# Linear attention: the output product of a tile seven turns after its projection, at the end of TensorE's turn, instead of eight turns after it, near the beginning

## What is computed

```python
q = jax.nn.elu(q) + 1.0
k = jax.nn.elu(k) + 1.0
kv = jnp.einsum('blhd,blhe->blhde', k, v)
kv_cumsum = jnp.cumsum(kv, axis=1)
k_cumsum = jnp.cumsum(k, axis=1)
out = jnp.einsum('blhd,blhde->blhe', q, kv_cumsum)
denom = jnp.clip(jnp.einsum('blhd,blhd->blh', q, k_cumsum), 1e-06, None)
out = out / denom[..., None]
return out.reshape(Bx, Lx, HIDDEN) @ Wo.T
```

## Time and profile before

| | us |
|---|---|
| median of 3 runs (3124.05 to 3134.37) | 3127.18 |
| the profiled execution, its own time | 3120.84 |
| span of its instructions | 3119.1 |
| TensorE busy, of the span | 2991.4 (96%) |
| VectorE busy | 2430.9 (78%) |
| ScalarE busy | 2056.4 (66%) |
| linear attention's turns, about | 438 to 710 |

### The profile page before, as it was taken

One profiled execution on the slowest core, in us unless ns is written; L12 is line 12 of the kernel. 1 busy time (PEld: TensorE's weight loads), 2 busy tenths in 40 slices (PEclk: granted clock), 3 DMA queues, 4 the chain that ended last, 5 costly groups with the idle time before them and its releaser, 6 DMA issues. The chain is left out here.

```text
span 3119.1 us, 62117 instructions
## 1 busy us (share of the span) xinstructions
PE 2991.4 (96%) x24364; PEld 1983.4 (64%) x24364; DVE 2430.9 (78%) x4816; ACT 2056.4 (66%) x3774; POOL 530.4 (17%) x608
## 2 busy tenths in 40 slices
PE   7999989998999989979999999999999999998998
PEld 6899978877899979964334333344333333344998
DVE  7533478966433589958988999999999999983887
ACT  5544545545644556642877888877888888877665
POOL 3322335543322422210000000000000000000222
PEclk9999999998999999988999999999999999999999
DMA  4211120002211200014104030300203030000000
GB/s 132 87 45 38 57 74 2 2 2 75 78 48 33 61 9 1 1 35 96 23 22 63 2 43 2 42 2 12 33 2 43 2 43 2 2 2 1 14 22 21
DMA packets 60113, 99.50 MB, mean 32 GB/s; under 512 B 7552, under 2 KB 43184, under 8 KB 57136
## 3 DMA queue, kind: packets, MB, share of 16 engines
q1 hardware_dynamic: 53488, 78.23, 11.5%
q0 software_dynamic: 6336, 17.31, 1.7%
HBM read 64.71 MB, written 30.67 MB: 31 GB/s over the span
## 5 line engine op out<-in xcount | busy, mean ns | idle before, releaser
L2427 DVE TENSOR_REDUCE smxp<-psum 128x1 f32<-128x512 f32 x2048 | 1257.8, 681 | 27.2 <-PE psum L2274 26.0
L2384 ACT ACTIVATE spr<-psum 128x512 f32<-128x512 f32 x2048 | 1114.8, 596 | 214.1 <-PE psum L2298 167.2
L2274 PE MATMUL psum<-sks,sqs 48*128 48x512 f32 x2048 | 761.6, 453 | 5.4 <-DVE spart L2419 3.0
L2298 PE MATMUL psum<-sqs,sks 50*128 50x512 f32 x2048 | 751.4, 451 | 0.0
L2315 PE MATMUL psum<-spr,sv 128*32 128x256 f32 x8192 | 656.1, 392 | 11.2 <-ACT sot L2393 8.9
L2274 PEld LDWEIGHTS psum<-sks,sqs 48*128 48x128 f32 x2048 | 311.3, 186 | 417.3 <-issue 391.6
L2315 PEld LDWEIGHTS psum<-spr,sv 128*32 128x32 f32 x8192 | 162.7, 108 | 379.6 <-ACT spr L2384 294.1
L2298 PEld LDWEIGHTS psum<-sqs,sks 50*128 50x128 f32 x2048 | 301.4, 185 | 15.9 <-issue 9.3
L1956 POOL MEMSET fhqb<- 128x64 f32 x3 | 0.3, 152 | 1480.8 <-POOLq L2184 1480.8
L579 PE MATMUL psum<-w_b,hsb_hi 128*128 (+1 forms) x1056 | 192.9, 281 | 0.7 <-DVE hsb_lo L837 0.7
L579 PE MATMUL psum<-w_a,hsa_hi 128*128 (+1 forms) x1056 | 192.9, 281 | 0.5 <-DVE hsa_lo L837 0.5
(11 more groups left out here) (412 smaller groups left out, 5809.6 us busy)
## 6 DMA issues: line engine op xcount, KB each, us to landing
sks<-q_parts SPq DMA_DIRECT2D x42, 256.0 KB, 9.2
sqs<-q_parts SPq DMA_DIRECT2D x42, 256.0 KB, 19.8
yo<-in_L_ffn_w_dram SPq DMA_DIRECT2D x32, 256.0 KB, 2.6
q_parts<-spart SPq DMA_DIRECT2D x16, 512.0 KB, 2.7
x<-in_L_attn_x_dram SPq DMA_DIRECT2D x8, 512.0 KB, 7.3
yo<-in_L_ffn_sw_dram SPq DMA_DIRECT2D x16, 256.0 KB, 3.0
xg<-f_sorted_a SPq DMA_DIRECT2D x8, 512.0 KB, 4.0
f_routed_a<-yo SPq DMA_DIRECT2D x8, 512.0 KB, 2.9
```

The costliest lines, as they stand in the source:

```text
L2274: e.matmul(bank(what), QS[n % 2][rows, pr, q0:q0 + P], KS[n % 2][rows, pr, jc * GW:(jc + 1) * GW], start=True, stop=True, tile_position=(H ...
L2298: e.matmul(out, KS[n % 2][rows, pr, jt * P:(jt + 1) * P], QS[n % 2][rows, pr, ic * GW:(ic + 1) * GW], start=True, stop=True, tile_position ...
L2384: e.activation(PR[j % 2][:, HEAD[i], :], src, ACT.Exp, scale=float(DH) ** -0.5).then_inc(*done.up)
L2427: e.tensor_reduce(out[:, pr, i, jc, a:a + 1], bank(what), AX.X, ALU.max).then_inc(*pm_free[use[what] % 4].up)
```

## The change

```diff
@@ -1387,8 +1387,6 @@
                                 divide_turn(n - 6)
                             if stage(n, 1):
                                 x_turn(n - 1)
-                            if stage(n, 8):
-                                output(n - 8)
                             if stage(n, 2):
                                 project(n - 2)
                             if stage(n, 5):
@@ -1409,6 +1407,8 @@
                             if stage(n, 4):
                                 scores(n - 4)
                             weights(n, True)
+                            if stage(n, 7):
+                                output(n - 7)
```

## The result

The changed kernel takes 3130.65 us in the median of 20 runs (3125.59 to 3144.39), the kernel before 3126.25 in 20 runs beside it. The ratio is 1.0025 with a 95% interval of 1.0015 to 1.0034, so by the ratio the change costs about 8 us of 3126, between 5 and 11. The medians themselves are only 4.4 us apart and the means 6.3, so timing alone gives the sign and little of the size. The forecast was a ratio of 1.0026, and "within 0.3%" was the likeliest case.

What follows compares the result with a forecast made beforehand. TensorE was taken to bound the kernel's projection turns. Chunk turns +6.3, turn 24 +0.4, turns 26 and 29 -1.5, plain turns +2.8, tail +0.2 sum to +8.2 us: 3135.4 us from a median of 3127.18, range 3126 to 3142.

Steps and rivals of the forecast that it cites:

- TensorE bounds this stage: Turns of the projection stage: TensorE busy 40 of 40 us, so its new waits are paid in full.
- The second rival: VectorE sets the pace; its 0.2 us wait at L1584 goes in 24 turns: -6.1, 3121.1 us; chance 0.05.
- Plain turns, +0.23: Border of each plain turn: 0.18 us stall for `aaoT_lo` plus 0.05 longer groups; 12 turns, 2.8 us.
- the 1.47 of the sum: Border between turns: output product 0.81, four transposes 0.44, `x_turn` 0.22; together 1.47 us, against 1.42 before.
- Chunk turns, a closed loop, +0.57: Turns 11 to 21: product, `x_turn`, ScalarE, VectorE back to `aaoT_lo`, 8.66 us against 8.09; 6.3 us in all.
- turn 24: Two VectorE operations on 704 columns, span 5.56: loop of 8.30 us against 7.91, so 0.39 more.
- Rival 1: VectorE makes up for its later start; only the wait by way of ScalarE stays: +4.2, 3131.4 us; chance 0.2.
- Rival 3: Loop longer than its parts: chunk spans at 6.09, plain turns +0.39; +11.9, 3139.1 us; chance 0.2.
- Rival 4: Wait isn't felt, as TensorE can't take the group before L1624 ends; -1.3, 3125.9 us; chance 0.05.
- Turns 26 and 29, -1.5: Ends of these turns: output product fills idle time while `x_turn` waits for `misc`; together 1.5 us gained.
- What costs nothing: Last turns, from 33 on: later product covered by waits for masks, but for 0.2 us in turn 37.
- Load ahead of a wait: Output product: weight loads not pulled ahead behind a wait; if they were, the sum would be 1.2 us less.

Runs made afterwards that it cites:

- e2: Against the kernel before: only the output products of tiles 19 and 22 moved, to the end of turns 26 and 29; ratio 1.0002.
- e3: Against the kernel before: only the output products of tiles 4 to 14 moved (ends of chunk turns 11 to 21); ratio 1.0012.
- e4: Against the kernel before: output products of all tiles but 4 to 14, 19 and 22 moved; ratio 1.0006.
- e1: Against the kernel before: the output product one place earlier, between `divide_turn` and `x_turn`; ratio 1.0003.
- e8: Against the changed kernel: `aao` transposed ahead of `qk_turn` in plain turns, ScalarE's copies swapped likewise; one execution 3150.24 us (kernel before 3139.61).
- e9: Against the changed kernel: `x_turn` of the next tile also at the turn's end, ahead of the output product; one execution 3139.74 us.
- e6: Against the changed kernel: one more VectorE copy of 128x256 in each of turns 11 to 21; one execution 3153.83 us (kernel before 3139.61).
- e7: Against the changed kernel: in turns 11 to 21 a weight chunk's last two VectorE operations behind the masks; one execution 3155.47 us (kernel before 3139.61).

## Why the prediction was right, and where its sum was off

- *TensorE bounds this stage.* Right. Every stall put at the border lengthened the turns, and e2, e3 and e4 add up to 5.71 of the 5.98 us. The second rival, VectorE as the pace, is out: its wait at L1584 went and nothing became faster. The share of VectorE's time (93%) was higher than that of the weight loads and yet told nothing of who waits for whom.
- *Plain turns, +0.23.* Right in size and parts: 0.25 to 0.26 measured (0.17 to 0.18 at the ends of turns 9 and 10), 0.19 of it the wait and 0.06 the border. The border's excess isn't where it was put: the groups up to `project` took 1.39 to 1.40 from the product's start, 0.07 less than the 1.47 of the sum and no more than the 1.42 before, and `project` 0.08 to 0.10 more than before. It takes 2.16 to 2.20 wherever it follows transposes (e1, e8 and e9 too) and 2.10 behind the output product; why, no run shows.
- *Chunk turns, a closed loop, +0.57.* The mechanism was right (e3, e6, e9); one term was mis-sized. The step from `x_turn` to L1468 was taken as 0.62 from the earlier trace rows; it measured 0.42. The prediction read it where ScalarE was still at work on the copies of `scores`:

```profile
469.68 1.09 ACT L1449 ACTIVATE aat<-psum 128x512 f32<-128x512 f32 x2 [0.45 <-PE psum L1360]
```

It held ScalarE until 470.77, and L1468 began at 470.66 as the next in the queue. The 0.62 was the end of that work, not the latency. The trace before also had rows in which ScalarE was idle: at the end of turn 26, L1468 starts at 626.42, 0.44 after `x_turn` at 625.98. After the change `x_turn` comes when ScalarE is idle ("0.47 <-PE psum L1301" above), and the loop is 0.82 + 0.44 + 0.42 + 0.41 + 5.90 + 0.41 + 0.06 = 8.46, which is the turn of these rows (8.49 is the mean of the eleven, 8.6 to 8.7 was forecast). The same 0.2 explains turn 24 (0.24 instead of 0.39), VectorE's wait at L1589 (0.6 instead of 0.8) and the product's lateness in chunk turns (0.24 to 0.50, mostly 0.3, instead of 0.5 to 0.6). The sum of the path was 2.1 us too high for it. The total came out at the forecast partly by luck: the timed difference of 7.8 has an interval of 3 us to either side, and the traces put it at 6.1 in these turns.
- *The other rivals.* Rival 1 (VectorE makes up for its later start) would have left chunk turns at 8.32; they took 8.49, and e6 shows the dose paid in full. Rival 3 (a longer span) is out: the span is 5.77 to 6.09 as before and plain turns grew by 0.25, not 0.39. Rival 4 is out by the product's wait of 0.19 in plain turns.
- *Turns 26 and 29, -1.5.* Right: -1.4, and e2 shows it alone.
- *What costs nothing.* Right: from turn 33 on, the tail grew by 0.1, where 0.2 was forecast.
- *Load ahead of a wait.* The prediction took the earlier trace rows to speak against a load pulled ahead behind a wait, since load and first matmul start together. That reading was too strong. In e8 the product waits for nothing, and yet its load and first matmul start together (486.12) and the group takes 0.81, against 0.82 behind a wait. So the wait adds at most 0.01 to the group, and whether the pulling ahead of which the Trainium skill speaks (TensorE: Matmul & The Clock Gate, Step-by-step: what each phase is for) also works behind a wait, no run here shows.

## What to carry to other kernels

A group that is moved up on the bounding engine must be checked against the end of what it waits for, to a tenth of a microsecond, and so must every group that it now stands in front of: what that group feeds can come back, a turn later, as the very thing waited for. Look for holes that have a cause elsewhere (a bank that is emptied late) and put independent work there only; moving it in all turns for the sake of two cost five times what those two gave back (7.4 us against 1.4). A latency read from a row is one only if the engine that takes up the work was idle before it.

## What the hardware showed beside that

The VectorE operations of e6 (a copy within SBUF) and e7 (two inputs in SBUF) hardly overlap with GpSimd's. Where the two meet in e6, one of them is held up: either the extra copy of 128x256 takes 1.35 to 1.39 us instead of 0.29, or GpSimd's operation takes 1.36 to 1.43 instead of about 1.28 (in turn 11, both):

```profile
533.10 1.26 POOL L1673 TENSOR_TENSOR aqe<-aqT,pair_mask 128x512 f32<-128x512 f32 x1 [4.15 <-ACT aqT L1494]
...
533.12 1.39 DVE L1620 TENSOR_SCALAR dose<-one_a 128x256 f32<-128x256 f32 x1
...
542.88 1.43 POOL L1673 TENSOR_TENSOR aqe<-aqT,pair_mask 128x512 f32<-128x512 f32 x1 [5.36 <-ACT aqT L1494]
...
542.89 0.29 DVE L1620 TENSOR_SCALAR dose<-one_a 128x256 f32<-128x256 f32 x1
```

The copy loses 1.10 us to an operation of 1.26, GpSimd's operation 0.15 to a copy of 0.29. The Trainium skill (SBUF — State Buffer, SBUF: two separate sides) describes an exclusive lock, held for the full instruction by whichever starts first, and no sharing of bandwidth. Such delays agree with it, and so does the copy that started 0.19 behind GpSimd's operation and took 1.35. With starts 0.02 apart the rows can't tell who was first: GpSimd's row leads by 0.02 at 533.10, where the copy lost, and by 0.02 at 587.24, where the copy took 0.29. The two operations of e7 stand in the kernel before where GpSimd is idle, and put behind the masks they took 2.4 us instead of 0.84.
